# A mixture-of-experts stage that runs 62 blocks of chosen token rows instead of 64 dense jobs

## What is computed

```python
x = x + xattn(layernorm(x), ctx_1024, ctx_1024)
x = x + selective_scan_layer(layernorm(x))
# MoE: 16 experts, 4 chosen for each token
h = layernorm(x)                                   # (1024, 512)
topk_idx, topk_weight = route(h)                   # (1024, 4)
combine = (one_hot(topk_idx, 16) * topk_weight[..., None]).sum(axis=1)
g = einsum('th,eih->tei', h, gate_proj)            # 16 experts, 256 x 512 each
u = einsum('th,eih->tei', h, up_proj)
expert_out = einsum('tei,ehi->teh', silu(g) * u, down_proj)
x = x + einsum('teh,te->th', expert_out, combine)
```

## Time and profile before

| | |
|---|---|
| median of 3 runs | 1513.53 us (1513.09 to 1516.65) |
| span of the profiled execution | 1514.9 us |
| TensorE busy | 1281.5 us, 85% |
| VectorE busy | 1157.1 us, 76% |
| ScalarE busy | 599.0 us, 40% |
| DMA moved | 128.47 MB, mean 85 GB/s |

### The profile page before, as it was taken

One profiled execution on the slowest core, in us unless ns is written; L12 is line 12 of the kernel. 1 busy time (PEld: TensorE's weight loads), 2 busy tenths in 40 slices (PEclk: granted clock), 3 DMA queues, 4 the chain that ended last, 5 costly groups with the idle time before them and its releaser, 6 DMA issues.

```text
span 1514.9 us, 16115 instructions
## 1 busy us (share of the span) xinstructions
PE 1281.5 (85%) x6400; PEld 965.9 (64%) x6400; DVE 1157.1 (76%) x1001; ACT 599.0 (40%) x1229; POOL 0.2 (0%) x4
## 2 busy tenths in 40 slices
PE   6998578868859758858758898999999999998998
PEld 4776446646536547536537586777777777676775
DVE  1201899998999998999998848979888888446554
ACT  4432754554655535745536611131313131022220
POOL 0000000000000000000000000000000000000000
PEclk9999878988978978979879789999999999999999
DMA  7333013324013324013314201222222312114553
GB/s 247 101 121 127 6 25 116 104 63 133 8 49 91 118 54 128 10 49 110 89 57 145 91 22 35 86 61 70 56 77 63 84 49 63 56 44 152 168 160 103
DMA packets 95930, 128.47 MB, mean 85 GB/s; under 512 B 4976, under 2 KB 70640, under 8 KB 95856
## 3 DMA queue, kind: packets, MB, share of 16 engines
q1 hardware_dynamic: 95856, 127.45, 27.9%
HBM read 125.21 MB, written 2.23 MB: 84 GB/s over the span
## 4 chain that ended last, share of the span: by engine, by line
DVE 55%; PE 31%; ACT 8%; issue 3%; DMA 2%; DVEq 0%; ACTq 0%; SPq 0%
DVE state L1077 16%; PE bank L634 11%; DVE y_acc L1084 8%; DVE state L1074 8%; DVE state L1080 7%; PE bank L591 6%; PE bank L665 6%; ACT decay L855 4%; DVE x_tokens L1179 3%; DVE w_lo L1161 2%; DMA queries_ctx<-in_dt_t 2%; PE bank L520 2%; PE bank L545 2%; DVE hidden L1168 2%; DVE hidden L1167 2%
## 5 line engine op out<-in xcount | busy, mean ns | idle before, releaser
L1077 DVE TENSOR_TENSOR_SCAN state<-decay,state 128x2048 f32<-128x2048 f32 x64 | 282.9, 4420 | 8.3 <-ACT decay L855 7.2
L665 PE MATMUL bank<-w_down,hidden 128*128 128x512 f32 x512 | 232.1, 596 | 5.2 <-DVE x_tokens L1179 5.2
L634 PE MATMUL bank<-x_hi,w_hi 128*128 128x256 f32 x1024 | 192.6, 312 | 12.2 <-DVE hidden L1168 7.5
L855 ACT ACTIVATE decay<-delta_odd,params 128x256 f32<-128x256 f32 x256 | 106.3, 498 | 197.7 <-DVE state L1077 186.8
L634 PEld LDWEIGHTS bank<-x_hi,w_hi 128*128 128x128 f32 x1024 | 150.3, 198 | 43.5 <-issue 30.4
L520 PE MATMUL bank<-ctx,queries_ctx 128*128 128x256 f32 x512 | 151.8, 449 | 22.2 <-ACT queries_ctx L748 22.2
L634 PE MATMUL bank<-x_hi,w_lo 128*128 128x256 f32 x1024 | 168.9, 288 | 0.0
L634 PE MATMUL bank<-x_lo,w_hi 128*128 128x256 f32 x1024 | 168.7, 288 | 0.0
L902 ACT ACTIVATE hidden<-bank 128x512 f32<-128x512 f32 x64 | 38.0, 594 | 327.6 <-PE bank L665 321.5
L665 PEld LDWEIGHTS bank<-w_down,hidden 128*128 128x128 f32 x512 | 93.3, 191 | 100.5 <-issue 94.2
L1084 DVE TENSOR_TENSOR y_acc<-y_acc,state 128x2048 f32<-128x2048 f32 x64 | 146.7, 2292 | 2.3
(11 more groups left out here) (128 smaller groups left out, 1328.1 us busy)
## 6 DMA issues: line engine op xcount, KB each, us to landing
ctx<-in_ctx_t SPq DMA_DIRECT2D x32, 512.0 KB, 6.3
ctx<-in_ctx_n SPq DMA_DIRECT2D x32, 512.0 KB, 3.5
bc_bcast<-bc_scratch SPq DMA_DIRECT2D x64, 256.0 KB, 5.1
raw_w<-in_eg_t SPq DMA_DIRECT2D x32, 512.0 KB, 4.3
raw_w<-in_eu_t SPq DMA_DIRECT2D x32, 512.0 KB, 4.0
w_down<-in_ed_t SPq DMA_DIRECT2D x32, 512.0 KB, 4.8
queries_ctx<-in_dt_t SPq DMA_DIRECT2D x4, 2048.0 KB, 10.0
queries_ctx<-in_xp_t SPq DMA_DIRECT2D x4, 2048.0 KB, 14.8
```

The source lines that it names most:

```text
L634: mm = pe.matmul(o, w[a](k), x[b](k), start=(q == 0), stop=(q == len(terms) - 1))
L665: mm = pe.matmul(b[t][:, :], hid[j % 2][:, i * GT + t * P:i * GT + (t + 1) * P], w_dn[k % 2][:, i, :], start=(i == 0), stop=(i == IC - 1))
L855: ins = act.activation(dA[n % 2][:, k * GT:(k + 1) * GT], dlt[g % 2][:, k, :], ACT.Exp, scale=par[:, c:c + 1])
L1077: dve.tensor_tensor_scan(h, dA[n % 2], h, 0.0, ALU.mult, ALU.add).then_inc(scan_rd, 1)
```

## The change

The MoE no longer computes all experts for all tokens. The router's choice is turned into row numbers on the core. Each token's normed row is written four times into a table in HBM, once into the region of each chosen expert (`dispatch`, indirect transfers issued by GpSimd). The table is then worked off in blocks of 128 rows of one expert. A block table made on VectorE (`slots`, `block_table`, `out_slots`) says which expert and which rows each block has; SyncE reads both into registers (`value_load`) and loads with computed addresses. The number of blocks is fixed at its upper bound: 39 for the first wave (groups 0 to 2) and 23 for the second (group 3), 62 in all, whatever the routing. Each block loads its own weights, gate, up and down, into one of three buffers (`NW` = 3).

For a block, TensorE transposes the 128 rows (four transposes), does gate and up together as four float32 matmuls of 512 columns, transposes the hidden activations (two) and does `down` as two float32 matmuls of 512 columns. The result is stored in a second HBM table. When a wave is complete, GpSimd gathers the four rows of each token back (`collect`) and VectorE adds them with their weights (`combine`). The rows of the dispatch table are set to zero beforehand, by 40 transfers of up to 512 rows (`CLEARS`), issued during the attention of groups 0 and 1.

The router of group 0 runs in the phase of group 1's scan, that of group 1 in the phase of group 2's scan, that of group 2 between group 3's projections and the first block. Group 3's scan runs beside the first 32 blocks, its output projection follows in step `OUT_STEP` = 31, and its routing in the steps after that. The splitting into two parts (`split_hi`, `split_lo`, `split_matmul`) is gone.

```diff
-PIECES = 2
-RAW = 5
-CA = G - 1
-JA = E * CA
-JOBS = JA + E
-SCAN_FROM = 4
-SCAN_JOBS = 39
-OUT_JOB = SCAN_FROM + SCAN_JOBS + 1
...
+WAVES = ((0, 1, 2), (3,))
+WAVE_OF = [w for g in range(NGR) for w in range(len(WAVES)) if g in WAVES[w]]
+WTILES = [[TILE0[g] + t for g in gs for t in range(NTS[g])] for gs in WAVES]
+CAP = [P * len(t) for t in WTILES]
+BLOCKS = [(TOPK * c + E * (P - 1)) // P for c in CAP]
+BLOCK0 = [sum(BLOCKS[:w]) for w in range(len(WAVES))]
+ROWS = [E * c + b * P - TOPK * c for c, b in zip(CAP, BLOCKS)]
+CLEAR_ROWS = 512
+CLEARS = [(w, r, min(r + CLEAR_ROWS, ROWS[w])) for w in range(len(WAVES)) for r in range(0, ROWS[w], CLEAR_ROWS)]
+CLEAR_UNITS = range(1, 15)
+NW = 3
+NX = 3
+REST = 8
+OUT_STEP = BLOCKS[0] - REST
...
+            def load_block_w(w, j):
+                q = BLOCK0[w] + j
+                sp.wait_ge(tab_rdy, w + 1)
+                e = sp.value_load(tabs[w][j:j + 1, 0:1], min_val=0, max_val=E - 1)
+                if q >= NW:
+                    sp.wait_ge(y_full, q - NW + 1)
+                for p, t in enumerate((eg_t, eu_t)):
+                    sp.dma_start(wb_[q % NW][:, p * DC * I:(p + 1) * DC * I],
+                                 t[bass.DynSlice(e, 1)].rearrange("o (p c) i -> p (o c i)", p=P)).then_inc(gu_in[q % NW], 16)
+                sp.dma_start(wb_[q % NW][:, 2 * DC * I:],
+                             ed_t[bass.DynSlice(e, 1)].rearrange("o (p c) d -> p (o c d)", p=P)).then_inc(dn_in[q % NW], 16)
+            def load_block_x(w, j):
+                q = BLOCK0[w] + j
+                if j == 0:
+                    sp.wait_ge(tab_rdy, w + 1)
+                    sp.wait_ge(dispatched, 16 * TOPK * sum(len(WTILES[v]) for v in range(w + 1)))
+                row = sp.value_load(tabs[w][j:j + 1, 1:2], min_val=0, max_val=ROWS[w] - P)
+                if q >= NX:
+                    sp.wait_ge(xt_full, q - NX + 1)
+                sp.dma_start(xb[q % NX], xd[w][bass.DynSlice(row, P)]).then_inc(xb_in[q % NX], 16)
+            def store_block_y(w, j):
+                q = BLOCK0[w] + j
+                sp.wait_ge(y_rdy, q + 1)
+                sp.dma_start(yd[w][j * P:(j + 1) * P], yb[q % NX]).then_inc(yb_out[q % NX], 16)
...
-            def load_raw(q):
-                if q < 2 * E * PIECES:
-                    if q >= RAW:
-                        sp.wait_ge(w_rdy, q - RAW + 1)
-                    elif q == 0:
...
+            for w in range(len(WAVES)):
+                for j in range(NW):
+                    load_block_w(w, j)
+                for j in range(NX):
+                    load_block_x(w, j)
+                for j in range(BLOCKS[w]):
+                    if j + NX < BLOCKS[w]:
+                        load_block_x(w, j + NX)
+                    if j + NW < BLOCKS[w]:
+                        load_block_w(w, j + NW)
+                    store_block_y(w, j)
+                    if w == 0:
+                        for q in ((-1, 0) if j == 0 else (j,)):
+                            for state, part in scan_parts(q):
+                                if part == SCAN_PARTS - 1 and state + 2 < NS:
+                                    load_bc((NGR - 1) * NS + state + 2)
...
+            def experts(w):
+                q0, n = BLOCK0[w], BLOCKS[w]
+                pe.wait_ge(d_free, jd.n)
+                for j in range(-2, n + 1):
+                    if j + 2 < n:
+                        block_x_t(q0 + j + 2)
+                    if 0 <= j + 1 < n:
+                        gate_up(q0 + j + 1)
+                    if 0 <= j - 1:
+                        down(q0 + j - 1)
+                    if 0 <= j < n:
+                        hidden_t(q0 + j)
+                    if w == 0 and j == OUT_STEP:
+                        pe.wait_ge(y_rdy, OUT_STEP)
+                        out_proj(NGR - 1)
+                    if w == 0 and j == OUT_STEP + 1:
+                        ffn_logits(NGR - 1)
+                    if w == 0 and j == OUT_STEP + 3:
+                        positions(NGR - 1)
...
+            def gate_up(q):
+                pe.wait_ge(xt_rdy, q + 1)
+                pe.wait_ge(gu_in[q % NW], 32 * (q // NW + 1))
+                if q >= 2:
+                    pe.wait_ge(h_rdy, q - 1)
+                o = bank[2 + q % 2][:, :].rearrange("p (g i) -> p g i", g=2)
+                for c in range(DC):
+                    mm = pe.matmul(o, xbT[q % 2][:, c, :], w_gu[q % NW][:, :, c, :], start=(c == 0), stop=(c == DC - 1))
+                mm.then_inc(gu_full, 1)
+            def down(q):
+                pe.wait_ge(a_free, ha.pop(q))
+                pe.wait_ge(dn_in[q % NW], 16 * (q // NW + 1))
+                if q >= 2:
+                    pe.wait_ge(y_rdy, q - 1)
...
-            def gate_up(j):
-                k, e, c = job(j)
-                b = x_pair(x_item(j))
-                if first_job(c) == j:
-                    pe.wait_ge(xm_rdy, c + 1)
-                x_parts = [(lambda q, v=v: v[:, q * GT:(q + 1) * GT]) for v in xm[c % CA]]
-                for p in range(PIECES):
-                    pe.wait_ge(w_rdy, k * PIECES + p + 1)
-                    for i in range(IC):
-                        w_parts = [(lambda q, v=v: v[p][:, q, i * P:(i + 1) * P]) for v in w_gu[k % 2]]
-                        mm = split_matmul(b[p][:, i * GT:(i + 1) * GT], w_parts, x_parts, DC)
-                mm.then_inc(x_full, 1)
...
+            def keep_y(q):
+                act.wait_ge(y_full, q + 1)
+                if q >= NX:
+                    act.wait_ge(yb_out[q % NX], 16 * (q // NX))
+                act.activation(yb[q % NX], bank[4 + q % 2][:, :], ACT.Copy).then_inc(y_rdy, 1)
...
+            def ffn_norm(c):
+                norm_stats(TILE0[c], NTS[c])
+                if c:
+                    dve.wait_ge(dispatched, 16 * TOPK * TILE0[c])
+                else:
+                    dve.wait_ge(cleared, 16 * len(CLEARS))
+                for t in range(NTS[c]):
+                    ins = dve.tensor_scalar(fx[:, t, :], xs[:, TILE0[c] + t, :], mv_[:, 2 * t:2 * t + 1],
+                                            rstd[:, t:t + 1], ALU.subtract, ALU.mult)
+                ins.then_inc(fx_rdy, 1)
+                dve.wait_ge(fx_rdy, c + 1)
...
+            scan_step(NGR - 1, 1)
+            route(NGR - 2)
+            slots(NGR - 2)
+            block_table(0)
+            out_slots(0)
+            for w in range(len(WAVES)):
+                q0, n = BLOCK0[w], BLOCKS[w]
+                for j in range(-1, n):
+                    if j + 1 < n:
+                        hidden(q0 + j + 1)
+                    if w == 0:
+                        for state, part in scan_parts(j):
+                            scan_step(NGR - 1, state, parts=(part,))
+                        if j == OUT_STEP:
+                            add_tiles(NGR - 1)
+                            ffn_norm(NGR - 1)
+                        if j == OUT_STEP + 1:
+                            route(NGR - 1)
+                        if j == OUT_STEP + 3:
+                            slots(NGR - 1)
+                            block_table(1)
+                            out_slots(1)
+                    elif j >= 2 and j % 2 == 0 and (j - 2) // 2 in range(len(WTILES[0])):
+                        combine((j - 2) // 2, WTILES[0][(j - 2) // 2])
+            for i, t in enumerate(WTILES[1]):
+                combine(len(WTILES[0]) + i, t)
...
+            for i, (w, first, end) in enumerate(CLEARS):
+                n = CLEAR_UNITS[i * len(CLEAR_UNITS) // len(CLEARS)]
+                pool.wait_ge(s_full, n)
+                v = xd[w][first:end].rearrange("(p r) d -> p r d", p=P)
+                pool.dma_start(v, fx_[:, 0:D].unsqueeze(1).to_broadcast([P, (end - first) // P, D])).then_inc(cleared, 16)
+            pool.wait_ge(cleared, 16 * len(CLEARS))
+            def dispatch(c):
+                pool.wait_ge(slot_rdy, c + 1)
+                for t in range(NTS[c]):
+                    for k in range(TOPK):
+                        i = (TILE0[c] + t) * TOPK + k
+                        pool.indirect_dma_start(xd[WAVE_OF[c]], bass.IndirectOffsetOnAxis(slot[:, i:i + 1].bitcast(U32), 0),
+                                                fx[:, t, :], None).then_inc(dispatched, 16)
+            def collect(n, w, t):
...
+            for c in range(NGR):
+                dispatch(c)
+            for w in range(len(WAVES)):
+                end = BLOCK0[w] + BLOCKS[w]
+                pool.wait_ge(yslot_rdy, w + 1)
+                for s in range(NX):
+                    pool.wait_ge(yb_out[s], 16 * len(range(s, end, NX)))
+                for i, t in enumerate(WTILES[w]):
+                    collect(w * len(WTILES[0]) + i, w, t)
```

More of the change, by code:

```diff
@@ L376, in load_down @@
[L376 to L387 removed]
+                g = k // NS
@@ L688, in _ @@
                 projections(g + 1)
-                if g + 2 < G:
-                    norm_transposes(NT, NT)
-                else:
-                    prepare(0)
```

(55 more changed lines are left out.)

1002 lines of the change are left out of this document (540 added, 462 removed).

## The result

The kernel after the change took 2023.7 us (median of 4 runs, 2021.4 to 2025.0) beside 1514.0 us before (4 runs, 1513.1 to 1516.7): the ratio is 1.336, with a 95% interval of 1.334 to 1.338. The direction was as forecast, the size was not: 1790 was predicted and 1905 was the top of the range. The profiled execution has a span of 2018.7 us.

A forecast was written before the change was run, and what follows sets the result against it. The prediction took a loop closed by each block's gate and up load, with a partly slow clock, to bound the MoE: 1039 us of fixed parts plus 56 periods of 13.4 us (750) gave 1789, rounded 1790; range 1625 to 1905 us.

The forecast's parts named there:

- the order of the loads: MoE blocks: each waits for its gate and up load after `down`; 13.4 us a block against 6.0 without the wait.
- C: Rival: TensorE at half clock in all blocks, or costly register addresses; 15.4 to 15.6 us a block, 1901 to 1913 us; chance 0.14.
- 1039: Forecast time in us outside the 56 block periods: start, first block, projection, change of waves, gathers and tail.
- TensorE's own work: One MoE block: 5.16 us of matmuls and 0.8 of transposes, 6.0 us in all at full clock.
- The clock: About 4.5 us of idle TensorE a block drops the granted clock to half, costing 2.9 us a block.
- Rival B: The load is on the path but the clock holds: 10.5 us a block, 1627 us; chance 0.14.
- The weight pair: Gate and up loads of a block, 512 KB each: 5.3 us with SyncE's wake, to the second landing.
- The load's address registers: Computed addresses of block loads: at most one more issue of 0.37 to 0.50 us for each of two, 6.3 us as upper bound.
- Part (1): Up to the end of group 3's scan inputs: 847 us before plus 33 for clears, norms and routing, 880.
- Part (2): From group 3's scan inputs to the first `y_full`, TensorE idle: 80 us, so 960.
- Parts (3) to (5): Both waves and tail: 56 periods, 5 us ending each wave, projection 9, second wave's start 33, gathers 3, tail 24.
- the profile after was to show: Blocks every 13 to 14 us, gate or up DMA waits of 3 to 4.5 us, TensorE near 60%, DMA 125 to 155 GB/s.

The follow-up runs named there:

- e1: The changed kernel with each block's rows loaded one block earlier, weights as they were; 1837.4 us, 1.213 of the kernel before.
- e3: The changed kernel with rows and gate and up weights both loaded two blocks earlier; 1465.6 us, 0.966 of the kernel before.
- e4: The changed kernel with 17 unused matmuls of 256 columns behind each `down`, to fill idle TensorE; 1950.9 us, 1.288 of the kernel before.
- f1: e3 with the clearing transfers spread over attention units from 9 on, not from 1 on; 1458.5 us, 0.963 of the kernel before.
- f5: e3 with late clears, second wave's loads early, first rows ahead of later weights, group 2's routing ahead of last scan's state 1; 1439.8 us.

## Why the prediction was wrong

**What failed** is one sentence in the part on the order of the loads: that the store of y and the load of x "are issued after them", are drained before the next load, and so lie off the loop. The first half is right and is the cause. The text had written down TensorE's order, "transposes of block j+2, `gate_up(j+1)`", and then followed only the weights through it. The rows that these transposes need are issued behind three weight loads and the store of y, all of which wait for the same `down`. So the loop is closed by the last transfer that the `down` releases. The terms, predicted and as the block above measured:

| term | predicted | measured |
|---|---|---|
| `down` ends to first issue | 0.1 | 0.2 |
| issues ahead of the one waited for | in the 5.3 | 2.5 |
| that transfer to landing | 5.2 (weights) | 6.1 (rows) |
| transposes of the rows | under the load | 1.1 |
| gate, up and down at the clock granted | 5.16 + 2.9 | 5.7 + 1.7 |
| sum (this block's) | 13.4 | 17.3 |

Over the 56 steps the mean of after is 17.02 us (618.1 us for 36 of them, less the 3.1 that the projection adds, and 338.4 for 20). 56 x 3.62 (17.02 - 13.4) is 203 of the 230 us. e1 shows both halves: with the rows alone taken off, the step is 13.7 and `gate_up` waits for weights, as the prediction had it.

**The bound.** The range ended at C, the load of the prediction at half clock throughout. No case had another transfer on the loop, so 17 lay outside of them all. The rows of before had the price of a rival "the rows land last": 0.1 us to wake, four issues at 0.45, 5.1 for 256 KB by itself, 0.5 for four transposes, 5.16 and 2.9 are 15.6 us, and 1039 + 56 x 15.6 = 1913 us. That is nearer, and still 1.4 us a step short of the 17.0 (1.7 of this block's 17.3: in a full queue the rows take 6.1 and not 5.1, and the register load 0.7).

**TensorE's own work** was right: 5.87 us in e3 against 6.0.

**The clock** was right in kind and near in size. `gate_up` takes 5.67 us in place of 3.44, 2.2 more, and the transposes 1.13 in place of 0.48: 2.9 together, as predicted, if on other instructions. The granted clock was 0.59 in that stretch, and the `down` behind it took its usual 1.73 us, so it rises within each block, and rival C does not hold. Rival B leaned on a reading of the earlier trace rows that was wrong: the 1.00 of 500.50 to 503.00 us is the clock during the idle time and not behind it. What came behind it in before:

```profile
503.13 0.66 PE L532 MATMUL bank<-params,probs 128*128 128x128 f32 x4 [2.72 <-ACT probs L768]
503.62 3.15 PE L520 MATMUL bank<-ctx,queries_ctx 128*128 128x256 f32 x8
```

Eight of the same take 1.99 us 4 us later, and the granted clock from 505 to 509 us is 0.68: it fell behind 2.72 us of idle time too. So a load with that little idle time would not have kept it up. The Trainium skill's TensorE: Matmul & The Clock Gate, section HAM oscillation, has each slice of such a loop begin slow; the trace agrees, with 46 of 62 `gate_up` at 5 us or more. e4 puts 1.8 to 2.5 us on it.

**The weight pair** was predicted with 5.3 us and is 5.3 in after by the medians and 5.45 in e1. The Trainium skill's DMA: Bandwidth & Descriptors, section Anatomy of one DMA, gives 4.4 us as an estimate, and with it a step of 12.6 in e1, whose step is 13.7: the row was the better price.

**The load's address registers** were bounded at up to one more issue each. They cost 0.7 us between the store of y and the rows (1132.93 to 1133.63), within what was taken.

**Part (1)**, to the last group's scan inputs: 880 predicted, 897.5 measured. The clears cost 20 us and not 10 (11.2 us to landing for `ctx`, 5.0 before). The second and third phases grew by 5.6 and 16.0 us, against 4.4 for one `ffn_norm` and 15.4 for one with a `route` and `slots`. The last grew by 9, against 3: if `route` and `slots` cost their 11 there too, taking the experts' preparation out gave back 2 of the 8 us.

**Part (2)**, to the first `y_full`: 80 predicted, 93.5 measured (897.5 to 991.0). The chain of after there:

```profile
949.24 0.96 POOL dispatched L1506
...
950.50 7.21 DMA dispatched<-ffn_x,slot
...
958.51 6.13 DMA block_x<-dispatched
...
966.74 4.17 PE bank L721 x8
...
978.99 3.30 ACT decay L974 x8
...
982.82 6.43 PE bank L721 x8
```

The scatters are 1.26 us apart (0.96 on GpSimd and 0.30 between), near the 1.5 taken, but the last needs 7.2 us to land, and all of it is on the path: the weights, which I had put there, lie beside it. From the rows' landing to the first `down`'s end it is 26 us and not 17: between the first `gate_up` and the second ScalarE first waits for the scan and runs the decays of a state, 12 us.

**Parts (3) to (5)**: the projection adds 3 us and not 9, being in a longer idle time. The waves part with 38.1 us from `down` to `down`, 33 predicted. The tail, from the last `down` (1997.3) to the end, is 21.4 us against 24.

Together: 31 us late at the first `y_full` (17.5 + 13.5), 203 in the steps, -6 for the projection, 2 for the last steps of the waves, 5 at the change of waves, -3 for the gathers, which cost nothing that shows, and -2.6 in the tail: 229 of 230.

**Of what the profile after was to show**: a wait ahead of `gate_up` once a block and a fallen clock behind it, yes; a DMA of gate or up as its cause, and 3 to 4.5 us of it, no. It is `block_x`, 8.65 us. DMA at 125 to 155 GB/s, yes (130 and 140), and it told nothing apart. TensorE busy near 60%, no: 50%.

## What to carry to other kernels

When buffers come free, write down every transfer that the same event releases, in the order in which the queue issues them, and for each the first instruction that needs it: the loop closes over the last transfer that anything ahead in the consumer's order waits for, small as it may be. Two such loops can lie side by side, and then neither cure alone shows its worth (186 and 161 us here, 558 for both with a second step of lead), so an experiment that removes one cause and gains a third is no proof against the other. With loads that run ahead of the work, and the fixed parts trimmed, this same change is 4.9% faster and not 34% slower.

## What the runs showed of the hardware that was not expected

- A transfer of 256 KB issued behind 1.75 MB took 6.1 us to land, 3.6 behind 0.75 MB: its place in the queue counts for more than its size.
- 1 MB transfers of GpSimd's queue beside SyncE's more than double the landing time of 512 KB loads in the first phase (11.2 us beside them, 5.0 before and 4.5 in f1 without them; 17.1 in f1's second phase), though SyncE issues them from a queue of its own.
- An indirect transfer of 128 rows (scatter) lands 5.6 us after its issue in the median, 7.2 for the last of a group's eight on the chain. What it costs GpSimd depends on VectorE: 0.96 us each, 1.26 apart, in groups 2 and 3 of after; 2.0 to 4.7 us, 2.8 in the mean, in groups 0 and 1, beside the scan (VectorE busy 24.7 of 25 us); and 3.0, 4.1 and 2.1 us for the three of f5 that were moved beside a scan state.
- An idle time of 2.72 us in before was followed by a granted clock of 0.68 from 505 to 509 us, so a wait need not be as long as the 8.65 us of after to cost clock.
- In the second wave of e3 DMA and TensorE are both full, at 388 GB/s and 5.87 us a block, and `gate_up` still takes its 3.44 us.
- 7.5 us of matmuls a block whose result nobody reads made the kernel 73 us faster; with them the granted clock was 0.97 to 0.99 in place of 0.7.
